# A fused attention and expert kernel: VectorE computes six quarters of a wavelength per unit in pieces of 2048 columns, TensorE adds a linear term in a second pass, and the head is rearranged

## What is computed

```python
def wl_step(acc, wl):
    cpm, iw = wl
    m = cpm[None, :, None, None]
    Qw = Q * m
    Kw = K * m
    scores = jnp.einsum('bhqd,bhkd->bhqk', Qw, Kw) * SCALE
    scores = scores * jnp.cos(KERR * scores * scores)
    attn = jax.nn.softmax(scores, axis=-1)
    out = jnp.einsum('bhqk,bhkd->bhqd', attn, V)
    return (acc + out * iw, None)
```

## Time and profile before

| | |
|---|---|
| median of 3 runs | 1771.12 us (1767.68 to 1771.59) |
| the profiled execution | 1770.11 us, span 1768.4 us |
| busy: ACT, DVE, PE, PEld, POOL | 97%, 88%, 84%, 54%, 10% of the span |
| mean granted TensorE clock | 0.991 |
| whole exponentials on ScalarE | 477 of 128 x 4096, 1676.2 us |
| VectorE's own exponentials | 119 quarters |

### The profile page before, as it was taken

How to read it: one execution, slowest core, us unless ns; L and a number is a source line. 1 busy time by engine, 2 the same in 40 slices (tenths; PEclk the granted TensorE clock), 3 DMA queues, 4 the chain that set the end, 5 groups by cost and what they waited for, 6 DMA issues and landing times.

```text
span 1768.4 us, 45997 instructions
## 1 busy us (share of the span) xinstructions
PE 1491.2 (84%) x20128; PEld 950.7 (54%) x20128; DVE 1558.5 (88%) x2447; ACT 1711.1 (97%) x520; POOL 173.3 (10%) x185
## 2 busy tenths in 40 slices
PE   5887888887788899999999987887788787788788
PEld 3454554554555566666666655554455555455555
DVE  4569889998888999999999998899988988988797
ACT  4898999999999999999999999999999999999996
POOL 4406000111110000000000000132220000000000
PEclk8999999999999999999999999999999999999999
DMA  3200000110001110011110000000000000000000
GB/s 121 94 21 15 15 2 33 52 51 26 20 14 36 36 44 28 30 31 43 44 43 23 15 10 15 25 24 26 26 9 15 15 15 15 15 7 11 2 28 26
DMA packets 45822, 49.63 MB, mean 28 GB/s; under 512 B 7564, under 2 KB 38324, under 8 KB 45620
## 3 DMA queue, kind: packets, MB, share of 16 engines
q1 hardware_dynamic: 42176, 42.11, 7.4%
q0 software_dynamic: 2048, 4.20, 0.8%
q10 hardware_dynamic: 1396, 0.33, 0.1%
HBM read 30.50 MB, written 15.73 MB: 26 GB/s over the span
## 4 chain that ended last, share of the span: by engine, by line
ACT 77%; PE 17%; issue 3%; DVE 1%; DMA 1%; SPq 0%; POOL 0%; DVEq 0%
ACT Pr L1323 77%; PE bank L1186 10%; PE bank L960 2%; PE bank_b L1282 1%; PE bank L1255 1%; PE bank L1117 0%; DMA base<-in_L_attn_x_dram 0%; PE bank L604 0%; PE bank L1101 0%; PE bank L548 0%; PE bank L574 0%; PE bank L499 0%; PE bank L489 0%; PE bank L953 0%; PE bank L1468 0%
## 5 line engine op out<-in xcount | busy, mean ns | idle before, releaser
L1323 ACT ACTIVATE Pr<-T 128x4096 f32<-128x4096 f32 x477 | 1676.2, 3603 | 15.1 <-PE bank L1186 12.4
L1186 PE MATMUL bank<-Pr,Vst 128*32 128x256 f32 x15360 | 931.3, 382 | 240.8 <-ACT Pr L1323 129.2
L1186 PEld LDWEIGHTS bank<-Pr,Vst 128*32 128x32 f32 x15360 | 515.7, 109 | 538.0 <-issue 333.8
L1123 DVE COPY T<-bank 128x512 f32<-128x512 f32 x248 | 169.2, 685 | 47.7 <-PE bank L1117 46.4
L1107 DVE TENSOR_REDUCE negmax<-bank 128x2 f32<-128x512 f32 x248 | 158.8, 681 | 16.9 <-PE bank L1101 16.8
L1238 DVE SCALAR_TENSOR_TENSOR shared<-d_mantissa,shared 128x1024 f32<-128x1024 f32 x119 | 150.0, 1261 | 2.8
L1235 DVE SCALAR_TENSOR_TENSOR shared<-shared,d_scaled 128x1024 f32<-128x1024 f32 x119 | 145.1, 1219 | 0.1
L1232 DVE SCALAR_TENSOR_TENSOR d_mantissa<-d_mantissa 128x1024 f32<-128x1024 f32 x119 | 144.8, 1217 | 0.0
L1230 DVE SCALAR_TENSOR_TENSOR shared<-d_mantissa 128x1024 f32<-128x1024 f32 x119 | 144.7, 1216 | 0.1
L1282 PE MATMUL bank_b<-terms,ident 128*128 128x128 f32 x992 | 143.7, 277 | 0.3 <-DVE terms L1267 0.3
L1248 DVE TENSOR_SCALAR pv_s<-bank,row_scale 128x512 f32<-128x512 f32 x192 | 142.2, 740 | 0.9 <-PE bank L1186 0.8
(11 more groups left out here) (230 smaller groups left out, 935.4 us busy)
## 6 DMA issues: line engine op xcount, KB each, us to landing
Ks<-qk_parts SPq DMA_DIRECT2D x30, 288.0 KB
Qs<-qk_parts SPq DMA_DIRECT2D x90, 96.0 KB
qk_parts<-work SPq DMA_DIRECT2D x12, 384.0 KB, 3.4
work<-in_L_ffn_w_dram SPq DMA_DIRECT2D x16, 256.0 KB, 3.6
dispatched<-d_scaled SPq DMA_DIRECT2D x5, 512.0 KB, 6.0
region<-dispatched SPq DMA_DIRECT2D x8, 320.0 KB, 3.6
expert_out<-work SPq DMA_DIRECT2D x8, 320.0 KB, 2.8
out_dram<-base SPq DMA_DIRECT2D x8, 256.0 KB, 2.6
```

What stands on the lines that cost most here:

```text
L1123: nc.vector.tensor_copy(T[par][:, ds(p * BANK, BANK)], sc_bank[rr][:, :]).then_inc(sc_read, 1)
L1186: ins = nc.tensor.matmul(bank[VC * j:VC * (j + 1), half * SEQ:(half + 1) * SEQ], Vst[par][:, at:at + VC], moving, start=opens and half == ...
L1323: nc.scalar.activation(Pr[n % RING][:, :], T[par][:, :], ACT.Exp, scale=scales[u % 2][w]).then_inc(exp_done, 1)
```

## The change

Fourteen plain units (6 to 8 and 18 to 28) become "wide". In these VectorE computes the last wavelength whole and the first half of wavelength 14, in three pieces of 2048 columns with six operations each. ScalarE's exponential of wavelength 14 covers 2048 columns. The exponential is made in another form: a scaled integer `y` read as a float is linear in the mantissa; TensorE multiplies `y` with V times a constant (`V_mant`) and in a second pass a cubic `z` with V (`V_one`). Both scaled copies of V are staged by GpSimd once per unit, after the last products of the unit before. Wide products gather in a bank of their own. `WIDE_OPS_AT` and `PASS_AT` deal operations and passes out over the steps. The bias is added in 32 operations of 128 columns. In the head TensorE runs filler matmuls on zeros while it waits for x; copies are shared between ScalarE and VectorE, and V's projections follow the scores of both halves.

```diff
+    PIECES = ((W - 1, 0, 2), (W - 1, 1, 2), (W - 2, 0, 2))
+    POPS = 6
...
+            def keep_clock(n, cols):
+                for _ in range(n):
+                    nc.tensor.matmul(banks[0][:, 0:cols], ident[:, :], zeros[:, 0:cols].bitcast(f32), start=True, stop=True)
             pe.wait_ge(const_ready, 3)
+            keep_clock(6, BANK)
+            pe.wait_ge(x_in[0], 16)
+            keep_clock(8, BANK)
+            pe.wait_ge(var_ready, 1)
+            keep_clock(5, SEQ)
             turn_x(0)
...
             spread_max(0)
             first_transposed(0)
-            pe.wait_ge(wv_in, 32)
-            pe_v(pe, 0)
             spread_max(1)
             first_transposed(1)
-            for n in range(1, NQ_SIDE):
+            pe.wait_ge(wv_in, 32)
+            for n in range(NQ_SIDE):
                 pe_v(pe, n)
...
+            act.wait_ge(nm_made, 1)
+            nc.scalar.activation(nm_wide[:, 0:SEQ], banks[5][:, 0:SEQ], ACT.Copy).then_inc(nm_spread, 1)
+            for b in (0, 2):
+                act.wait_ge(t0_made, b + 1)
+                nc.scalar.activation(T[0][:, b * BANK:(b + 1) * BANK], T0_LOW[b][:, :], ACT.Copy).then_inc(t0_low, 1)
         def head_vector(dve):
+            for b in (1, 3):
+                dve.wait_ge(t0_made, b + 1)
+                nc.vector.tensor_copy(T[0][:, b * BANK:(b + 1) * BANK], T0_LOW[b][:, :]).then_inc(t0_low_v, 1)
+            dve.wait_ge(nm_made, 2)
+            nc.vector.tensor_copy(nm_wide[:, SEQ:2 * SEQ], banks[2][:, 0:SEQ]).then_inc(nm_spread, 1)
+            for b in range(HALF_B):
+                dve.wait_ge(t0_made, HALF_B + b + 1)
+                nc.vector.tensor_copy(T[0][:, (HALF_B + b) * BANK:(HALF_B + b + 1) * BANK], T0_HIGH[b][:, :]).then_inc(t0_high, 1)
             dve.wait_ge(wv_in, 32)
             dve_v(dve, 0)
             dve_v(dve, 1)
...
-                for c in range(CHUNKS):
-                    b = base[:, c * CH:(c + 1) * CH, :]
-                    nc.gpsimd.tensor_tensor(b, b, bo_s[:, :].unsqueeze(1).to_broadcast([P, CH, D]), ALU.add).then_inc(biased, 1)
+                for t in range(TILES):
+                    nc.gpsimd.tensor_tensor(base[:, t, :], base[:, t, :], bo_s[:, :], ALU.add).then_inc(biased, 1)
...
+            def pe_pass(pe, u, i, final):
+                w, half, tiles = PIECES[i]
+                bank = x_bank[u % 2]
+                if (i, final) == (0, 0):
+                    pe.wait_ge(wide_staged, 2 * (WIDE_BEFORE[u] + 1))
...
+                pe.wait_ge(d_step, D_OPS_BEFORE[u] + POPS * i + (POPS if final else 1))
+                source, V = ((wide_y, V_mant), (wide_z, V_one))[final]
...
+            def dve_wide(dve, u, n):
...
+                    ins = nc.vector.tensor_scalar(y.bitcast(i32).rearrange("p (j r) -> p j r", j=GR), src, scale, -LIFT * MANT, ALU.mult, ALU.add)
+                elif op == 1:
+                    dve.wait_ge(d_step, made + 1)
+                    ins = nc.vector.tensor_scalar(m.bitcast(i32), y.bitcast(i32), 0x007FFFFF, 0x3F800000, ALU.bitwise_and, ALU.bitwise_or)
+                elif op == 2:
+                    dve.wait_ge(d_step, made + 2)
+                    ins = nc.vector.scalar_tensor_tensor(m, m, r_, m, ALU.add, ALU.mult)
+                elif op == 3:
+                    dve.wait_ge(d_step, made + 3)
+                    ins = nc.vector.scalar_tensor_tensor(m, m, s_, m, ALU.add, ALU.mult)
+                elif op == 4:
+                    if i:
+                        dve.wait_ge(pass_done, passes + 2 * i)
+                    elif KINDS[u - 1] == WIDE:
+                        dve.wait_ge(whole_done, WHOLE_BEFORE[u])
+                    ins = nc.vector.tensor_scalar(z.bitcast(i32), y.bitcast(i32), 0x7F800000, None, ALU.bitwise_and)
+                else:
+                    dve.wait_ge(d_step, made + 5)
+                    ins = nc.vector.scalar_tensor_tensor(z, m, q_, z, ALU.add, ALU.mult)
...
+                if w == W - 2 and KINDS[u] == WIDE:
+                    to, blocks = (t[:, :].rearrange("p (j b k) -> p j b k", j=GR, k=SEQ)[:, :, PIECES[-1][2]:, :] for t in (Pr[n % RING], T[par]))
...
+            def stage_wide(pool, u):
+                all_products_done(pool, u - 1)
+                pool.wait_ge(wide_clear, 4)
+                for v, factor in ((V_one, V_DOWN), (V_mant, -MANT_PART * V_DOWN)):
+                    nc.gpsimd.tensor_scalar(wide_blocks(v)[:, :, 0:HD], Vall[:, ds(u * SIDE_TILES * HD, SIDE_TILES * HD)]
+                                            .rearrange("p (t d) -> p t d", d=HD), factor, None, ALU.mult).then_inc(wide_staged, 1)
...
+            WIDE_OPS_AT = (1, 1, 1, 0, 0, 2, 1, 2, 1, 1, 1, 2, 2, 2, 1, 0)
+            PASS_AT = {3: ((0, 0),), 8: ((0, 1),), 9: ((1, 0),), 12: ((1, 1),), 13: ((2, 0),)}
```

More of the change, by code:

```diff
@@ L101, in attention_and_experts @@
         token_row = sb("token_row", [P, TILES])
-        wq_s, wk_s, wv_s, wo_s = (sb(n, [P, D]) for n in ("wq_s", "wk_s", "wv_s", "wo_s"))
+        early = sb("early", [P, 5 * D])
+        wq_s, wk_s, wv_s, bv_s, bo_s = (early[:, i * D:(i + 1) * D] for i in range(5))
+        wo_s = sb("wo_s", [P, D])
         bq_s, bk_s = sb("bq_s", [P, 1]), sb("bk_s", [P, 1])
-        bv_s, bo_s = sb("bv_s", [P, D]), sb("bo_s", [P, D])
         gw_s = sb("gw_s", [P, E])
@@ L1189, in pe_products, with wide_product @@
                 ins.then_inc(whole_done if by_vector == ALL_CHUNKS else pv_done, 1)
+            wide_y = shared[:, 0:2, :].rearrange("p c k -> p (c k)")
+            wide_z = shared[:, 2:4, :].rearrange("p c k -> p (c k)")
+            wide_m = d_both[:, :]
+            def wide_product(pe, bank, w, half, kt, V, moving, opens=False, closes=False):
+                for j in range(GR):
+                    blk = (2 * j + half) * QT + kt
+                    at = LEAD + blk * VC - (w - FIRST_OF[GROUPS - 1]) * OC
+                    ins = nc.tensor.matmul(bank[VC * j:VC * (j + 1), half * SEQ:(half + 1) * SEQ], V[:, at:at + VC], moving(j, blk),
+                                           start=opens, stop=closes)
+                return ins
@@ new lines, in pe_pass @@
+            def pe_pass(pe, u, i, final):
[3 more added lines that the diff above has]
+                    pe.wait_ge(wide_staged, 2 * (WIDE_BEFORE[u] + 1))
+                    pe.wait_ge(pv_copied, (u - 1) * GROUPS + 2)
+                    pe.wait_ge(x_read, X0 if u < EU else XO)
+                pe.wait_ge(d_step, D_OPS_BEFORE[u] + POPS * i + (POPS if final else 1))
+                source, V = ((wide_y, V_mant), (wide_z, V_one))[final]
+                last = final and i == len(PIECES) - 1
+                for kt in range(tiles):
+                    ins = wide_product(pe, bank, w, half, kt, V, lambda j, blk: source[:, (j * tiles + kt) * SEQ:(j * tiles + kt + 1) * SEQ],
+                                       opens=(i, final, kt) == (0, 0, 0), closes=bool(last and kt == tiles - 1))
+                ins.then_inc(whole_done if last else pass_done, 1)
@@ L1369, in attention_and_experts @@
             LONG_BEFORE = before([W - (c > 0) - (u == 0) for u, c in enumerate(D_CHUNKS)])
-            CHUNKS_BEFORE = before(D_CHUNKS)
+            D_OPS_BEFORE = before([POPS * len(PIECES) if k == WIDE else DOPS * c for k, c in zip(KINDS, D_CHUNKS)])
+            WIDE_BEFORE = before([k == WIDE for k in KINDS])
             WHOLE_BEFORE = before([c == ALL_CHUNKS for c in D_CHUNKS])
@@ L1572, in unit @@
                                 pool_combine(pool, c // 2)
+                        if half == 0 and KINDS[u + 1] == WIDE:
+                            if not WIDE_BEFORE[u + 1]:
+                                clear_wide(pool)
+                            stage_wide(pool, u + 1)
                 CU = EU + E + 1
```

130 lines of the change are left out of this document (95 added, 35 removed).

## The result

The changed kernel takes 1761.45 us (median; 1759.01 to 1764.27) where the kernel before took 1771.36 beside it: ratio 0.9948, 95% interval 0.9932 to 0.9964. It is faster, as forecast, and inside the range; but 9.9 us came where 19 were forecast. The profiled execution took 1764.27 us (span 1762.4), the longest of the four.

What follows compares the result with a forecast made beforehand. ScalarE's exponentials were taken to bound the kernel, at 52.6 us a plain unit. Wide units 9.0, bias 6.5 and head 3.0 us sum to 18.5, from 1770.1 to 1751.6, predicted as 1752 us; range 1742 to 1765.

Steps and rivals of the forecast that it cites:

- The wide unit itself: Each of 14 wide units: 51.5 us, 1.1 less than before, 15.4 us in all, with VectorE at its limit.
- the ring's wait: Wide units: the two-buffer ring of exponentials makes ScalarE wait 0.33 us for wavelength 13's products; 51.3 us a unit.
- the staging: Two more GpSimd operations of 128x128 per unit for the second pass: 0.1 us each charged, bounds nothing and 0.3 each.
- the old quarters: VectorE's old work in a unit: 6.4 us a quarter, 25.8 for four, leaving 20.6 for the rest.
- Combining: Four units where GpSimd combines the experts' results: VectorE loses 1.6 us in each, no longer hidden, adding 6.4 us.
- TensorE at nothing, the tightest step is 12: Wide units: 24 more matmuls, at most 2.9 us, hidden under ScalarE; step 12 fullest at 3.5 of 3.51 us.
- Bias: Unit 2: cutting the bias additions into 32 pieces shortens ScalarE's 7.09 us stall, gaining 6.5 us; bounds 5 and 7.1.
- nothing is late next: After the bias cut in unit 2, nothing else is late until the following unit.
- Head: Start of the kernel: fillers and new order gain some 3 us, bounds -1 and 7; first products near 49.5 us.
- VectorE as the bound in earnest: Rival, chance 0.2: wide units take 52.4 us, ScalarE idles in each, 6.1 us won in all, 1765 us.
- The clock does not hold in the head: Rival judged, chance 0.2: fillers keep TensorE's clock full in the head, 4 to 6 us more gained, 1747 us.
- VectorE kept its fast pace: Rival judged, chance 0.05: VectorE's scaling loses the fast pace, wide units take 54.7 us, 1797 us in all.

Runs made afterwards that it cites:

- head alone: The changed kernel with all units plain and the bias in four long operations, leaving only the new head: 1769.5 us, ratio 0.9986.
- bias alone: The kernel before with only the bias cut into 32 pieces: 1764.3 us, ratio 0.9965.
- the run with the paced bias: The changed kernel with the 32 bias additions moved from unit 2 into unit 3, two to an exponential: 1760.7 us, ratio 0.9941.
- combination in pieces: The changed kernel with each combination cut into 8 multiplications and 8 additions of 128 columns: 1752.5 us, ratio 0.9894.

## Why the prediction was right or wrong

- *The wide unit itself: right, in part by luck.* 51.45 us for 51.5, the ring's wait 0.40 for 0.33, VectorE at 98%. The operations of 2048 columns took 2.28 and 1.22 us, as worked out, and the staging cost nothing that shows. But 51.5 was VectorE's sum, and VectorE is busy 50.2: 10.15 us a piece for 10.3, and 19.7 for the rest, which the prediction had at 20.6 because it took off 25.8 us for the old quarters (26.6 by the trace). What sets the unit is ScalarE with the ring's wait, for which the prediction had 51.3.
- *Combining: this step failed.* The prediction charged what VectorE loses in a plain unit, 1.6 us, four times, 6.4 us, as if a unit grew by what VectorE loses and no more. VectorE lost 2.05, the units grew by 3.05: 12.2 us. VectorE's loss is the trigger; the rest is TensorE's in-order wait for what VectorE makes late and half its clock behind it. Taking the combining's work out gave 11 us back.
- *"TensorE at nothing, the tightest step is 12": wrong place.* The sum of matmuls per step was right (44.37 us busy for 44.9), but at step 15 TensorE waits for VectorE's copy even in a quiet unit. In two units without combining the clock fell there, 2.9 us in all in the profiled execution. I had looked for late products, not for what TensorE waits for in order.
- Together the wide units, forecast at 9.0 us, gave almost nothing: 9.9 less 2.2 (head alone) and 7.1 (bias alone) leaves 0.6 by the medians, with some 4 us of uncertainty from the three intervals. In the two profiled executions, from unit 6 on, it is 0.7. What the combining units cost over the forecast (12.2 less 6.4) and the 2.9 us of the two others account for the loss.
- *Bias: somewhat too high.* 6.5 us were forecast, and 7.1 came alone by the medians (the interval is 3.7 to 8.5). But from unit 1 to unit 6, where it acts, the profiles show 5.5 us where the clock holds and 3.8 in the changed kernel, where it falls. A short addition took 0.52 us for the 0.3 worked out, and "nothing is late next" was wrong: 1.1 to 2.8 us of stall stayed.
- *Head: right in the sum* (3.0; 2.2 alone, interval 0.7 to 4.1), by two errors against each other. The fillers were charged 0.5 us at the first maxima and cost 2.6; without them the head gains 4.7 (2.2 and 2.5), so the new order gives more than I gave it. The first products start at 49.86 us, for 49.5.
- *The rivals.* VectorE as the bound in earnest came at the time it names (1765 against 1761), but not by its mechanism: quiet units are at 51.45, not 52.4. The clock does not hold in the head. VectorE kept its fast pace (1.28 us for the scaling).

## What to carry to other kernels

A spare engine's slack is a buffer against everything that disturbs it: spend it to 98% and each disturbance that was free comes due, with whatever waits in order behind it. So price a disturbance by the waits that it meets after the change, not by the busy time that it adds before the change. Beside a busy VectorE, give GpSimd short instructions or units that have room; and put work ahead of a critical start only if it ends before that start.

## What the runs showed of the hardware that was not expected

- TensorE's granted clock fell to 0.50 behind single waits inside units in which it is busy 86% of the time. The length of the wait does not settle it alone. At step 15 the clock fell behind each of the twelve waits of 3.06 us (the changed kernel, the run with the paced bias, the one without fillers); behind the wait of 1.94 us at the start of unit 19 in four of six profiles; behind one of four waits of 2.18 to 2.31 us (combination in pieces); and behind few of the many waits of 1.75 to 1.78. Near 179 us it fell behind the same 0.85 us in four of eight profiles, with the same code up to there on TensorE, apart from the head.
- GpSimd's multiplications and additions of 128 columns took 0.96 and 1.19 us each on average beside a VectorE busy to 98%, 17.2 us for what two long ones did in 7.5, and yet took less from VectorE: 0.5 us for 2.05.
